# Moving the fold and the tent of 24 of 32 tiles from VectorE to ScalarE in a deformable-convolution kernel

## What is computed

```python
x = x + _L0_conv_ref(_gn(x), W, b)                    # all-pairs mixing of pixels
x = x + _L1_conv_ref(_gn(x), w1, b1, w2, b2, wd)      # deformable convolution

def _L0_conv_ref(x, W, b):                            # x: 4 x 128 x 32 x 32
    xn = xf / jnp.maximum(norm, EPS)
    s = jax.nn.relu(jnp.einsum('bcp,bcq->bpq', xn, xn)) ** GAMMA
    gx = jnp.einsum('oc,bcp->bop', W, xf) + b[None, :, None]
    y = jnp.einsum('bpq,bcq->bcp', s, gx)

def _L1_conv_ref(x, w1, b1, w2, b2, wd):
    offset = conv2d_same(conv2d_same(xd, w1, b1), w2, b2)
    return jax.nn.relu(deform_conv(x, offset, wd, k=3, pad=1, dg=4))
```

## Time and profile before

| what | value |
|---|---|
| median of 3 runs | 460.2 us (459.57 to 460.83) |
| the profiled execution | 459.05 us, span 457.0 us, mean granted TensorE clock 0.97 |
| TensorE busy | 405.2 us, 89% of the span |
| VectorE busy | 339.5 us, 74% |
| ScalarE busy | 215.6 us, 47% |
| GpSimd busy | 90.0 us, 20% |
| chain that ended last | TensorE 46%, VectorE 32%, DMA 6%, ScalarE 4% |

### The profile page before, as it was taken

The page is one execution under the profiler, slowest core; times in us unless marked ns, Lnnn a source line. Parts: engine busy times, 40 slices in busy tenths (PEclk is TensorE's granted clock), DMA queues, the critical chain, the costliest instruction groups (busy, mean ns, idle before and its releaser), DMA issues.

```text
span 457.0 us, 9689 instructions
## 1 busy us (share of the span) xinstructions
PE 405.2 (89%) x3887; PEld 291.9 (64%) x3887; DVE 339.5 (74%) x586; ACT 215.6 (47%) x392; POOL 90.0 (20%) x99
## 2 busy tenths in 40 slices
PE   6698989979998789799999798989869898979996
PEld 6455557646665565678666575768556566857875
DVE  5995776829999999388854999376979945779901
ACT  3343254345555365441655446331845643257661
POOL 5444470001774100000546100000010000000000
PEclk9899999999999899999999899989979997999999
DMA  7200002250011124332001313442213243303330
GB/s 252 77 0 0 0 2 75 84 141 1 2 47 46 47 67 146 85 90 91 12 13 36 92 54 94 124 126 81 59 47 100 90 122 98 104 23 107 96 105 24
DMA packets 46157, 32.71 MB, mean 72 GB/s; under 512 B 3264, under 2 KB 43488, under 8 KB 46112
## 3 DMA queue, kind: packets, MB, share of 16 engines
q1 hardware_dynamic: 46048, 31.95, 23.5%
q10 hardware_dynamic: 64, 0.13, 0.1%
HBM read 25.24 MB, written 10.37 MB: 78 GB/s over the span
## 4 chain that ended last, share of the span: by engine, by line
PE 46%; DVE 32%; DMA 6%; SPq 5%; issue 4%; ACT 4%; POOL 1%; DVEq 0%; ACTq 0%; POOLq 0%
PE psB L788 10%; PE psB L555 9%; PE psT L739 7%; DVE wpix L1507 7%; PE psV L762 5%; DVE combo L1294 4%; PE psA L646 4%; DMA h_scr<-h_ring 3%; SPq L320 3%; DVE combo_p L1298 2%; DVE tent L1488 2%; PE psA L555 2%; DVE tent L1482 2%; PE psB L813 2%; PE psA L813 2%
## 5 line engine op out<-in xcount | busy, mean ns | idle before, releaser
L1021 ACT ACTIVATE wcell<-psT 128x512 f32<-128x512 f32 (+1 forms) x160 | 83.9, 552 | 70.2 <-PE psT L739 68.9
L1507 DVE TENSOR_TENSOR wpix<-tent 128x512 f32<-128x512 f32 (+1 forms) x160 | 99.7, 675 | 14.4 <-PE psT L739 13.3
L739 PE MATMUL psT<-ident,wpix 128*128 128x128 f32 x576 | 89.1, 288 | 12.4 <-ACT wcell L1021 12.0
L739 PEld LDWEIGHTS psT<-ident,wpix 128*128 128x128 f32 x576 | 68.8, 148 | 37.2 <-issue 29.5
L493 POOL TENSOR_TENSOR sim<-rel 128x512 f32<-128x512 f32 x48 | 61.4, 1299 | 69.0 <-ACT rel L978 69.0
L1045 ACT ACTIVATE val<-psV 128x576 f32<-128x576 f32 x64 | 44.0, 688 | 30.7 <-PE psV L762 30.2
L788 PE MATMUL psB<-val,wd_sb 128*128 128x256 f32 x216 | 51.2, 392 | 0.0
L762 PE MATMUL psV<-wcell,hwin 64*32 64x144 f32 x2048 | 47.2, 294 | 3.9 <-ACT val L1045 3.5
L646 PE MATMUL psA<-sim,scratch 128*128 128x512 f32 x96 | 45.6, 597 | 0.6 <-POOL sim L493 0.6
L788 PEld LDWEIGHTS psB<-val,wd_sb 128*128 128x128 f32 x216 | 40.7, 193 | 8.3 <-issue 2.9
L555 PE MATMUL psB<-g_p 128*128 128x512 f32 x144 | 40.9, 419 | 0.0
(11 more groups left out here) (193 smaller groups left out, 453.6 us busy)
## 6 DMA issues: line engine op xcount, KB each, us to landing
hwin<-h_scr SPq DMA_DIRECT2D x128, 128.0 KB, 2.9
h_scr<-h_ring SPq DMA_DIRECT2D x8, 576.0 KB
h_ring<-sim SPq DMA_DIRECT2D x4, 512.0 KB
x_all<-x SPq DMA_DIRECT2D x1, 1536.0 KB, 10.0
out<-yout SPq DMA_DIRECT2D x12, 128.0 KB, 1.8
off_scr<-sim SPq DMA_DIRECT2D x4, 288.0 KB
combo<-sim SPq DMA_DIRECT2D x32, 32.0 KB
val<-w SPq DMA_DIRECT2D x1, 576.0 KB, 6.1
```

The costliest lines, as they stand in the source:

```text
L739: last = pe.transpose(bank[:, at:at + P], wpix[:, t % 2, k, 2 * h:2 * h + 2, :].rearrange("p g q -> p (g q)"), ident[:, :])
L1021: act.activation(wcell[:, t % 2, taps[0]:taps[-1] + 1, :, :].rearrange("q k h p -> q (k h p)"), bank[:, 0:len(taps) * G // 2 * P], ACT.Cop ...
L1507: dve.tensor_tensor(w, ty, tx, ALU.mult).then_inc(s["weights_done"], 1)
```

## The change

The tile `tent` gets a second buffer. `tents` on VectorE is split into `distances` and `tents`. For every tile but the first two of batch 0 and the last six of batch 3 (`by_vector`), ScalarE does what VectorE's `tents` did, as Abs and as Relu of 1 - |d|, at steps given by `TENT_AT` and, for tiles 0 and 1 of the next batch, `NEXT_TENTS`. VectorE's distances for these tiles get steps of their own (`DIST_AT`), ahead of the products by about one tile; those of a next batch's tiles 0 and 1 stand at step 67, and that batch's products of tile 0 move from step 67 to 71. TensorE's, GpSimd's and SP's instructions keep their order.

```diff
-        tent = sb("tent", [P, NOFF, SUP])
+        tent = sb("tent", [P, 2, NOFF, SUP])
...
-        LEAD_WEIGHTS, FIRST_WEIGHTS, LEAD_EXTREMES = 60, 67, 12
+        LEAD_WEIGHTS, FIRST_WEIGHTS, NEXT_WEIGHTS, LEAD_EXTREMES = 60, 67, 71, 12
+        DIST_AT = {3: 0, 4: 9, 5: 18, 6: 31, 7: 38}
+        TENT_AT = {2: 0, 3: 3, 4: 12, 5: 21, 6: 34, 7: 41}
+        NEXT_TENTS = {68: 0, 69: 1}
...
+        def by_vector(b, t):
+
+            return b == LAST and t >= 2 or b == 0 and t < 2
...
+            def tents(b, t):
+
+                n = ROWT * b + t
+                own = tent[:, t % 2, :, :]
+                act.wait_ge(s["dist_done"], n + 1)
+                act.activation(own, own, ACT.Abs).then_inc(s["fold_done"], 1)
+                act.wait_ge(s["fold_done"], n + 1)
+                act.activation(own, own, ACT.Relu, scale=-1.0, bias=ones[:, 0:1]).then_inc(s["tent_done"], 1)
+
...
+                        for tile, slot in TENT_AT.items():
+                            if slot == n and not by_vector(b, tile):
+                                tents(b, tile)
+                        if nxt is not None and n in NEXT_TENTS:
+                            tents(nxt, NEXT_TENTS[n])
...
-            def tents(b, t):
+            def distances(b, t):
...
-                if n > 0:
-                    dve.wait_ge(s["weights_done"], len(TAPS) * n)
-                else:
+                if n >= 2:
+                    dve.wait_ge(s["weights_done"], len(TAPS) * (n - 1))
+                if n == 0:
                     dve.wait_ge(s["cells_ready"], CELL_STEPS)
...
+            def tents(b, t):
+
+                n = ROWT * b + t
+                own = tent[:, t % 2, :, :]
                 dve.wait_ge(s["dist_done"], n + 1)
...
                 if i == 0:
-                    tents(b, t)
+                    if by_vector(b, t):
+                        distances(b, t)
+                        tents(b, t)
                     dve.wait_ge(s["tent_done"], ROWT * b + t + 1)
...
+                        for tile, slot in DIST_AT.items():
+                            if slot == n and not by_vector(b, tile):
+                                distances(b, tile)
                         if nxt is not None and n == FIRST_WEIGHTS:
+                            for tile in range(2):
+                                distances(nxt, tile)
+                        if nxt is not None and n == NEXT_WEIGHTS:
                             for i in range(len(TAPS)):
                                 weights(nxt, 0, i)
...
                 add_out(b, 0)
-                if nxt is not None:
-                    for i in range(len(TAPS)):
-                        weights(nxt, 1, i)
+                if not by_vector(nxt, 2):
+                    distances(nxt, 2)
+                for i in range(len(TAPS)):
+                    weights(nxt, 1, i)
...
             for i in range(len(TAPS)):
                 weights(0, 1, i)
+            distances(0, 2)
```

More of the change, by code:

```diff
@@ L185, in mix_deform_kernel @@
         edge = sb("edge", [P, SUP + 3])
-        place = tent[:, 0:NOFF // SUP, :].rearrange("p a b -> p (a b)")
+        place = tent[:, 0, 0:NOFF // SUP, :].rearrange("p a b -> p (a b)")
         tent_y, tent_x, wide_tmp = (raw[:, i * GK * WID:(i + 1) * GK * WID].rearrange("p (n r) -> p n r", r=WID)
@@ L1476, in tents @@
                     dve.wait_ge(s["pos_done"], 4 * b + t // 2 + 1)
-                if n > 0:
-                    dve.wait_ge(s["weights_done"], len(TAPS) * n)
-                else:
+                if n >= 2:
+                    dve.wait_ge(s["weights_done"], len(TAPS) * (n - 1))
+                if n == 0:
                     dve.wait_ge(s["cells_ready"], CELL_STEPS)
                 table = cells[:, 0 if t == 0 else 2 if t == ROWT - 1 else 1, :, :, :]
-                dve.tensor_tensor(tent[:, :, :].rearrange("p (k g a) r -> p k g a r", k=K, g=G),
+                dve.tensor_tensor(tent[:, t % 2, :, :].rearrange("p (k g a) r -> p k g a r", k=K, g=G),
                                   pos[:, t, :].rearrange("p (k g a) -> p k g a", k=K, g=G).unsqueeze(4)
@@ L1486, in tents @@
                                   ALU.subtract).then_inc(s["dist_done"], 1)
+            def tents(b, t):
+                n = ROWT * b + t
+                own = tent[:, t % 2, :, :]
                 dve.wait_ge(s["dist_done"], n + 1)
-                dve.scalar_tensor_tensor(out=tent[:, :, :], in0=tent[:, :, :], scalar=-1.0, in1=tent[:, :, :],
+                dve.scalar_tensor_tensor(out=own, in0=own, scalar=-1.0, in1=own,
                                          op0=ALU.mult, op1=ALU.min).then_inc(s["fold_done"], 1)
                 dve.wait_ge(s["fold_done"], n + 1)
-                dve.tensor_scalar(tent[:, :, :], tent[:, :, :], 1.0, 0.0, ALU.add, ALU.max)\
-                    .then_inc(s["tent_done"], 1)
+                dve.tensor_scalar(own, own, 1.0, 0.0, ALU.add, ALU.max).then_inc(s["tent_done"], 1)
             def weights(b, t, i):
                 if i == 0:
-                    tents(b, t)
+                    if by_vector(b, t):
+                        distances(b, t)
+                        tents(b, t)
                     dve.wait_ge(s["tent_done"], ROWT * b + t + 1)
@@ L1502, in weights @@
                 lo, hi = G * TAPS[i][0], G * (TAPS[i][-1] + 1)
-                tv = tent[:, :, :].rearrange("p (m a) r -> p m a r", a=2)[:, lo:hi]
+                tv = tent[:, t % 2, :, :].rearrange("p (m a) r -> p m a r", a=2)[:, lo:hi]
                 ty = tv[:, :, 0, :].unsqueeze(3).to_broadcast([P, hi - lo, SUP, SUP])
```

## The result

| | before | after |
|---|---|---|
| median of the runs, us | 460.3 (459.6 to 460.8) | 476.6 (475.0 to 478.6) |
| ratio, 95% interval | | 1.036 [1.032, 1.040] |
| profiled execution, us | 459.05, span 457.0 | 475.02, span 473.2 |

The change made the kernel 3.6% slower: 476.6 us, where 470.0 was forecast and 475.0 was the upper end of the range. The direction and nearly every wait came as forecast. What failed is the price of the later waits: only the first was given one for TensorE's clock behind it.

A forecast was written before the change was run, and what follows sets the result against it. TensorE was taken as the bound on average, with VectorE holding it up in batch 2. Six terms summed to +9.8 us on 459.05: 468.9, or 470.0 by the median; range 461.5 to 475.

The forecast's parts named there:

- Term 1: Start of batch 0: ScalarE's pair for tile 2 waits for VectorE's distances, so TensorE's first mix begins 8.3 us later.
- the pair's price: One Abs and one Relu of 576 columns on ScalarE: 1.46 us, scaled from similar rows, against 1.22 on VectorE.
- Term 2: Batch 0, behind the pause before the first mix: TensorE's granted clock is low for a while, +3.0 us.
- Terms 3 and 4: VectorE's lateness in batch 0 goes, -2.4 us; TensorE's waits for sample copies in batches 0 and 1 go, -1.4.
- term 4: Convolutions of batches 0 and 1: TensorE's two waits of 0.7 us for ScalarE's sample copy go, -1.4 us.
- Term 5: Ends of batches 0, 1 and 2: next batch's pairs on ScalarE delay TensorE's sample, +2.6, +2.0 and +0.2, together +4.8 us.
- the 2 to 3 named as a sign: Sign of a right forecast: at each of the first two batches' ends TensorE waits 2 to 3 us for a sample copy.
- Term 6: Batch 2: VectorE gets ahead of varp, TensorE's wait of 4.33 us shrinks; -2.5 us, since pairs stand between ScalarE's copies.
- ScalarE finds the distances ready: Rival, tile 2 of batch 0: distances end before ScalarE asks; 453.9 us, or 458.7 with the ends paid; chance 0.09.
- Both engines equally on the path: Rival, all 24 pairs: no wait decides, only their longer time on ScalarE, 5.8 us, giving 466.0; chance 0.05.

## Why the prediction was wrong, point by point

- **Term 1 (+8.3) and the pair's price (1.46)** were right: 8.2 and 1.46. The order of ScalarE's instructions and one duration of VectorE were enough. That POOL would be quiet during the stall was right too (0.00 us of work from 115 to 118).
- **Term 2 (+3.0)** was right in kind: 2.4.
- **Terms 3 and 4 in batch 0 (-2.4, -0.7)** were right, -3.1. In batch 1 term 4 gave nothing: TensorE lost its wait of 0.7 us for the sample and got one of 0.75 for a wcell copy shortly ahead of it.
- **Term 5 (+4.8)** had right how much later the samples would begin, 2.8, 1.9 and 0.2 us, though at the end of batch 1 TensorE waited 1.14 us for the copy and not the 2 to 3 named as a sign. It is **the step that failed**: "TensorE works without a pause from there on, so nothing is given back." Nothing was given back, but the wait also cost the clock behind it, 3.0 us more than its own length at the end of batch 0. The prediction had priced that in term 2 for one pause of 8 us and left it out for one of 2.7. The wait of 2.69 us that both kernels have got no price either, since it doesn't change; the clock behind it cost 2.8 us in this execution. Together that is 5.8 of the 6.4 us by which the sum was short. The 3.0 are the change's. Whether the 2.8 are is not shown: the control without a pair on ScalarE lost 1.2 there, and that the kernel before lost nothing in its traced execution may be luck.
- **Term 6 (-2.5)** had its mechanism right, the wait for varp went, but not its size. The pairs between ScalarE's copies put new waits of 1.24 and 2.02 us into TensorE's first turns, and a low clock behind them. With the end of batch 2 it came to -0.5 for -2.3.
- **The rivals.** "ScalarE finds the distances ready" named the right condition: where the order lets them be ready, all 24 pairs on ScalarE are a gain, 457.4 us and down to 451.5. Its own sum of 458.7, with only the first wait gone and the ends paid, no run shows: the nearest, the pairs of tiles 2 and 3 later, came to 470.0, with new waits for distances. "Both engines equally on the path" fell with these runs. The rule that stood behind it (the Trainium skill, page "ScalarE: Activation LUTs", section "Rules for kernel authors": relu and the like belong on VectorE) holds for the duration, 1.46 for 1.22, but did not decide the time here: VectorE was the one that was waited for in batch 2.
- **The range** had 3 us for the clock, once. With one more such drop at its upper end, 478, it would have held the median.

What stays open: why TensorE keeps the high clock behind the wait of 2.69 us in one execution and not in another. Only one execution of each kernel was traced. The times alone don't tell: the four of the changed kernel spread over 3.5 us, about one such drop, but the kernel before, 1.3 us in its own four, went from 457.4 to 465.0 beside the experiments.

## What to carry to other kernels

A wait of TensorE, where it bounds a kernel, is worth its length and what its clock loses behind it; here a wait of 2.7 us cost about twice its length, and work without a purpose in the wait won back the second half, not the wait itself. Before work is moved to an engine that executes in order, ask at each place whether its input is there when the engine comes to it: the same 24 pairs made the kernel 3.6% slower in one order and 1.8% faster in another. A duration read during a stall is that of a quiet machine; take the stall away and the neighbours are back.

## What the runs showed of the hardware

- In the changed kernel TensorE's granted clock was 0.50 over the 3.5 to 4.0 us behind waits of 2.69 and 2.72 us and of 2.02 behind one of 1.24. Behind the wait of 2.69 us it was 1.00 in the profile of before, and in the control, whose wait is 2.68, 0.66 from 189.2 to 193.0. The changed kernel did the twelve products behind a wait of 1.14 us in 2.86, the time they take at 1.00.
- 24 transposes in such a wait took 2.78 us, and the clock behind it was 1.00.
- VectorE's five products took 2.83 us with POOL idle, whether TensorE and ScalarE worked or not, and 5.24 us with POOL at its squares; two squares took 2.03 and 5.32.
